# Experts' outputs made beside the row gather, and the gated sum of them fused into the stage that computes the gates

## The reference

```python
h = (x_flat @ W_gat).reshape(M, HEADS, NUM_EXPERTS)          # 4 heads x 4 experts
e = leaky_relu(a_src[src] + a_dst[dst], negative_slope=0.2)
ee = exp(e - e_max[dst]); alpha = ee / (denom[dst] + 1e-16)
agg = segment_sum(h[src] * alpha[:, :, None], dst) + b_gat
scores = layernorm(agg, ln_gamma, ln_beta).reshape(M, HEADS, NUM_EXPERTS).mean(1)
topk_s, topk_i = top_k(scores, 2); w = softmax(topk_s)
for ei in range(4):
    g = where(topk_i == ei, w, 0.0).sum(-1)
    hh = gelu(x @ W1[ei] + b1[ei])                             # 128 -> 256
    out = out + g[..., None] * (hh @ W2[ei] + b2[ei])          # 256 -> 128
```

## Time and profile before

| | us |
|---|---|
| median of 3 runs (19387.88 to 19430.43) | 19410.53 |
| profiled execution, first to last instruction (span) | 20574.0 |

### The profile page before, as it was taken

How to read it: one execution, slowest core, us unless ns; L and a number is a source line. 1 busy time by engine, 2 the same in 40 slices (tenths; PEclk the granted TensorE clock), 3 DMA queues, 4 the chain that set the end, 5 groups by cost and what they waited for, 6 DMA issues and landing times. The chain is left out here.

```text
span 20574.0 us, 221676 instructions
## 1 busy us (share of the span) xinstructions
PE 6617.7 (32%) x79074; PEld 3179.5 (15%) x79074; DVE 7802.0 (38%) x10945; ACT 3746.9 (18%) x6493; POOL 10631.0 (52%) x10003
## 2 busy tenths in 40 slices
PE   0298411000000000099799998720000000000079
PEld 0133210000000000043255554310000000000034
DVE  9987495110011111344588886411111110111244
ACT  0132210000000000034766665510000000000023
POOL 0023687777777777622100000367777777777710
PEclk9599655555555555599899999855555555555589
DMA  1011201211111111155211113421111111111145
GB/s 41 18 43 47 74 14 49 49 38 35 35 38 38 38 38 38 17 143 121 68 47 45 45 47 96 133 56 38 38 38 38 38 35 38 35 38 38 26 103 130
DMA packets 866809, 1073.12 MB, mean 52 GB/s; under 512 B 353908, under 2 KB 570069, under 8 KB 846421
## 3 DMA queue, kind: packets, MB, share of 16 engines
q1 hardware_dynamic: 413908, 612.28, 10.5%
q0 software_dynamic: 328768, 179.97, 6.5%
q10 hardware_dynamic: 123456, 270.60, 3.8%
HBM read 671.93 MB, written 390.08 MB: 52 GB/s over the span
## 5 line engine op out<-in xcount | busy, mean ns | idle before, releaser
L956 POOL DMA_INDIRECT g_got<-table,g_ring x8192 | 8981.6, 1096 | 2705.2 <-issue 2674.8
L1178 PE MATMUL g_rowsP<-g_eye,g_meta 128*20 128x128 f32 x12 | 2.9, 416 | 10731.0 <-DVEq L1222 10731.0
L1070 DVE TENSOR_TENSOR g_z<-g_gs,g_adm 128x512 f32<-128x512 f32 x64 | 44.0, 688 | 8585.4 <-DMA g_gs<-rows 7831.9
L1033 ACT ACTIVATE g_low<-g_z 128x512 f32<-128x512 f32 x64 | 38.5, 601 | 10365.5 <-issue 7495.1
L1178 PEld LDWEIGHTS g_rowsP<-g_eye,g_meta 128*20 128x20 f32 x12 | 1.5, 142 | 10731.6 <-DVEq L1222 10731.2
L2132 POOL DMA_DIRECT2D m_x<-x x64 | 34.4, 537 | 2457.6 <-issue 2451.2
L1419 PE MATMUL f_hP<-f_xn,f_w 128*128 128x512 f32 x2048 | 965.8, 594 | 647.9 <-DMA f_xn<-xn 647.9
L1426 PE MATMUL f_oP<-f_hid,f_w 128*128 128x512 f32 x2048 | 962.1, 592 | 0.0
L1450 ACT ACTIVATE f_hid<-f_hP,f_b 128x512 f32<-128x512 f32 x1024 | 648.7, 685 | 1120.4 <-PE f_hP L1419 1020.2
L1466 DVE SCALAR_TENSOR_TENSOR f_part<-f_oP,f_b,f_gate 128x512 f32<-128x512 f32 x512 | 384.6, 751 | 970.7 <-PE f_oP L1426 970.7
L905 POOL DMA_INDIRECT ad<-h_hs,k_start_row x512 | 503.4, 983 | 341.5 <-ACT h_hs L889 178.1
(11 more groups left out here) (412 smaller groups left out, 16112.7 us busy)
## 6 DMA issues: line engine op xcount, KB each, us to landing
g_got<-table,g_ring POOLq DMA_INDIRECT x8192
f_gate<-gates SPq DMA_DIRECT2D x128, 1024.0 KB
rows<-g_got SPq DMA_DIRECT2D x512, 192.0 KB
g_gs<-rows ACTq DMA_DIRECT2D x64, 1536.0 KB
state<-g_out ACTq DMA_DIRECT2D x64, 1536.0 KB
h_x<-x SPq DMA_DIRECT2D x128, 256.0 KB
xn<-h_xn ACTq DMA_DIRECT2D x128, 256.0 KB
f_xn<-xn SPq DMA_DIRECT2D x128, 256.0 KB
```

Source lines behind the costliest of these rows:

```text
L956: pool.indirect_dma_start(self.got[:,par,k,:],None,self.table,bass.IndirectOffsetOnAxis(ap=self.ring[:,par,k:k+1].bitcast(u32),axis=0)).th ...
```

## The change

A class `Experts` makes, beside the gather, the outputs of all four experts for every token, plus the bias, token-major, and stores them to a DRAM tensor `ffn` [32768, 512]. Each of the 32 slots of the gather does two expert tiles ahead of the gather tile on TensorE, ScalarE and VectorE; in layer 0 TensorE waits for the end of the sort. The totals stage then also loads `ffn` and x (three tiles ahead, SyncE), scales each 128 x 128 block by its gate on ScalarE, sums the four by matmuls against the identity in PSUM, adds x on VectorE and stores the result. Tiles are interleaved with the gate groups: group 0, tiles 0 to 3, group 1, tiles 4 to 19, group 2, tiles 20 to 35, group 3, tiles 36 to 63. The stage `experts` is gone, and with it the store and the broadcast loads of the gates. Token order within the totals changes to node = n x 128 + p, so the load of `nodes` is now of 96-byte rows and is issued from ScalarE's queue; `Bounds` transposes three tables instead of one, and for layer 1 it moves from the experts stage into the mamba core, as 128 turns of two.

```diff
+class Experts:
+    def tensor(self,pe,t,par,first):
+        for u in range(EX*2):
+            e,f=u//2,u%2
+            if not (first and u<2): pe.wait_ge(self.active,t*EX*2+u-1)
+            TE.matmul(self.hP[:,f,:],self.w1[:,e,f*P:f*P+P],self.xs[:,par,:],start=True,stop=True).then_inc(self.up,1)
+        pe.wait_ge(self.active,t*EX*2+EX*2)
+        for q in range(BLOCKS):
+            if not (first and q<2): pe.wait_ge(self.biased,t*BLOCKS+q-1)
+            for e in range(EX):
+                for f in range(2):
+                    last=TE.matmul(self.oP[:,q%2,e*P:e*P+P],self.hid[:,e,f,q*P:q*P+P],self.w2[:,e,f,:],start=(f==0),stop=(f==1),skip_group_check=True)
+            last.then_inc(self.down,1)
+    def vector(self,dve,t,par,early):
+        for q in range(BLOCKS):
+            dve.wait_ge(self.down,t*BLOCKS+q+1)
+            self.nc.vector.tensor_tensor(self.y[:,par,q,:],self.oP[:,q%2,:],self.b2[:,:],ALU.add).then_inc(self.biased,1)
...
+                def experts(i):
+                    for k in range(2):
+                        ex.scalar(act,i*2+k,k,begin and k==0)
+                        if not (begin and k==0): ex.store(act,i*2+k-1,1-k)
...
                 def tile(i,par):
+                    experts(i)
...
+            def tiles(body, group):
+                group(0)
+                for t in range(TILES):
+                    if t%GT==GT//4 and t//GT+1<HI//GROUP: group(t//GT+1)
+                    body(t)
...
+                for t in range(TILES):
+                    sp.wait_ge(added,t+1)
+                    sp.dma_start(x_out[:,t*T:(t+1)*T],xo[:,t%2,:]).then_inc(x_put[t%2],16)
+                    if t+AHEAD<TILES: load(t+AHEAD)
...
+                    for q in range(BLOCKS):
+                        j=t*BLOCKS+q
+                        pe.wait_ge(gated,j+1)
+                        for e in range(EX):
+                            last=nc.tensor.matmul(mixP[t%2][:,q*P:q*P+P],part[:,j%2,e,:],ident[:,:],start=(e==0),stop=(e==EX-1),skip_group_check=True)
+                        last.then_inc(mixed,1)
...
+                        if j>=2: act.wait_ge(mixed,j-1)
+                        for e in range(EX):
+                            last=nc.scalar.activation(part[:,j%2,e,:],yin[:,t%AHEAD,q,e*P:e*P+P],ACT.Copy,scale=gt[:,e,j:j+1])
+                        last.then_inc(gated,1)
...
+                def add(t):
+                    dve.wait_ge(mixed,(t+1)*BLOCKS)
+                    V.tensor_tensor(xo[:,t%2,:],mixP[t%2][:,:],xin[:,t%AHEAD,:],ALU.add).then_inc(added,1)
-def experts(nc, x, xn, gates, w1, b1, w2, b2, x_out, beside=None, tag="f"):
-                sp.dma_start(gt[:,par,:,:],gates[:,bass.ds(i*T,T)].partition_broadcast(P)).then_inc(g_in[par],16)
```

More of the change, by code:

```diff
@@ L918 @@
 GROUP=64
+EX=4
+FF=256
+BLOCKS=T//P
 class Gather:
@@ L968, in attention @@
+def attention(nc, keep, src, dst, ad, table, rows_d, state_d, bgat, gamma, beta, eye, x, xn, w1, b1, w2, b2, ffn, x_out, beside=None, tag="g"):
     with ExitStack() as ctx0:
@@ L1005, in attention, with slots @@
             str_=state_d.rearrange("(p c) f -> p c f",p=P)
+            def slots(eng, body):
+                for i in range(2): body(i,i)
+                with eng.Fori(1,N//2-1) as t:
+                    body(t*2,0)
+                    body(t*2+1,1)
+                for i in range(N-2,N): body(i,i%2)
             block=ctx.enter_context(nc.Block())
@@ L1042, in tile @@
                     nc.scalar.dma_start(str_[:,bass.ds(i*C,C),:],out[:,par,1:C+1,:]).then_inc(out_in[par],16)
-                paired(act,N,tile,peel=True)
+                slots(act,tile)
+                ex.store(act,TILES-1,1)
+                ex.stored(act)
+                act.wait_ge(nodes_in,16)
                 for s in out_in: act.wait_ge(s,N//2*16)
@@ L1093, in tile, with _ @@
                     summed.of(dve,i)
-                paired(dve,N,tile,peel=True)
+                slots(dve,tile)
                 V.tensor_copy(tail[:,:],out[:,1,C,:])
-            if order: block.tensor(order.tensor)
+            @block.tensor
+            def _(pe):
+                if order:
+                    order.tensor(pe)
+                    pe.wait_ge(ordered,1)
+                pe.wait_ge(ex.w_in,64)
+                def tile(i,par):
+                    for k in range(2): ex.tensor(pe,i*2+k,k,isinstance(i,int) and i==0 and k==0)
+                slots(pe,tile)
         with ExitStack() as ctx:
@@ L1140, in attention @@
             movedP=[r.pb(f"movedP{k}",[P,2,HI]) for k in range(2)]
+            AHEAD=3
+            yin=r.sb("yin",[P,AHEAD,BLOCKS,EX*P])
+            xin=r.sb("xin",[P,AHEAD,T])
+            part=r.sb("part",[P,2,EX,P])
+            xo=r.sb("xo",[P,2,T])
+            mixP=[r.pb(f"mixP{k}",[P,T]) for k in range(2)]
+            y_in=[r.sem(f"y_in{k}") for k in range(AHEAD)]
+            x_in=[r.sem(f"x_in{k}") for k in range(AHEAD)]
+            x_put=r.pair("x_put")
+            gated,mixed,added=r.sem("gated"),r.sem("mixed"),r.sem("added")
             p_in=r.sem("p_in")
@@ L1197, in _, with group @@
                 go(row[:,5:7,:],row[:,5:7,:],ACT.Exp)
-                for q in range(HI//GROUP):
+                def group(q):
                     go(x3[:,:,:,:],x3[:,:,:,:],ACT.Exp)
@@ L1650, in mamba_core @@
         YO=r.pb("YO",[P,T])
+        bounds=beside(Room(nc,ctx,tag+"b"),GP[:,0:3*P].rearrange("p (a b) -> p a b",b=P))
         w_in=r.sem("w_in")
@@ L1815, in _ @@
             by_image(pe,step)
+            bounds.tensor_shift(pe)
+            bounds.tensor_end(pe)
         @block.scalar
```

262 lines of the change are left out of this document (104 added, 158 removed).

## The result

The changed kernel takes 18091.39 us, median of 4 runs (18069.7 to 18103.26); the kernel before took 19399.21 in 4 runs beside it (19375.07 to 19430.43). The ratio is 0.9324, with a 95% interval of 0.9311 to 0.9338: 1308 us less, where 1067 were forecast.

What follows compares the result with a forecast made beforehand. Each stage has its own limit: POOL's fetches in the gathers, TensorE in the experts stages. Experts -1790, totals +588, gathers +75 and core +60 sum to -1067, from 19410.5 to about 18345 us, range 18020 to 18880.

Steps and rivals of the forecast that it cites:

- the likeliest case: Whole kernel: the forecast of about 18345 us itself, own range 18070 to 18750, 71 in 100.
- What bounds each stage: Gathers are set by POOL's fetches, experts stages by TensorE, totals paced by fetches; core is near TensorE's and VectorE's limits.
- Room in the slot: Gathers: two expert tiles plus the gather tile take some 107 us, under the 180 us of 128 fetches.
- Guests and fetches, +75: Both gathers: added stores and loads slow the fetches, 71 us, plus 4 for `nodes`; from 0 to twice +75.
- The +527 of the rival: Gathers: 512 bias additions on VectorE hold up fetches as the sort does, +527 us, 18870; 6 in 100.
- Totals, +588: Both totals: 136 us of groups, 64 tiles of 6.0 us and 8, 528 against 234 us, +294 a layer.
- the first of the three candidates: Totals: ScalarE as a tile's limit, 16 operations of 0.254 us, 4.1 us a tile.
- The core, +60: Mamba core: 128 `Bounds` turns add VectorE work and fetches hold it up, partly hidden; +60 us, 0 to 205.
- Sum and surplus: Whole kernel: terms sum to -1067 us, with the 1163.5 us of profiled span over median left unchanged.
- a tile at 5.2 us (not 10.9): Totals, rival: ScalarE and TensorE take turns, 10.9 us a tile instead of 6.0, +627, 18970; 8 in 100.
- The better case: Totals and core: a tile at 4.9 us or less and a hidden core, 18070 and below; 6 in 100.
- the slot could turn the sign: Gathers, rival: a slot over 180 us costs 64 us per us, gain gone at 197; 3 in 100.

Runs made afterwards that it cites:

- before_again: The kernel before, unchanged, profiled a second time: run 19433.25 us, profile span 19431.7 us.
- adds_psum: The changed kernel with four unused 128x512 VectorE additions, one operand in PSUM, ahead of each bias addition: 18079.47 us, ratio 0.9325.
- stores_twice: The changed kernel with each `ffn` tile stored a second time, to a DRAM tensor nothing reads: 18092.73 us, ratio 0.9326.
- split_ahead: The changed kernel with one of four scalings moved from ScalarE to VectorE and four load buffers instead of three: 18022.85 us, ratio 0.929.
- core_alone: The kernel before with only layer 1's `Bounds` moved from the experts stage into the mamba core: 19405.44 us against 19399.28, ratio 1.0004.
- room_over: The changed kernel with 28 unused additions, one operand in PSUM, ahead of each bias addition: 20008.73 us, ratio 1.0316.
- split: The changed kernel with one of each four scalings done by VectorE instead of ScalarE, three load buffers: 18146.71 us, ratio 0.9353.

## Why the prediction was right, and where its sizes were off

The time lies in the range, and in the likeliest case's own range (18070 to 18750), but only 21 us above its lower end. Every cost was put too high and none too low, so no two errors cancelled. The steps, with the windows' bounds between gather and totals and otherwise from a stage's first to its last instruction, against the second profile of before (19431.7 to 18098.8, a change of -1333):

| step | forecast | measured |
|---|---|---|
| experts stages removed | -1790 | -1794 |
| totals | +588 | +441 |
| gathers | +75 | +17 |
| core | +60 | +18 |
| rest | 0 | -15 |
| sum | -1067 | -1333 |

- **What bounds each stage.** Right. That TensorE's 882 us disappear in POOL's gather is shown by its window and by the unchanged fetch.
- **Room in the slot.** The mechanism was right, its size too large: 107 us were forecast, 55 for the experts' matmuls and 52 for the gather tile's chain. With a backlog, just after the sort, the state stores of the changed kernel lie 59 us apart. This is its ScalarE timeline there, and TensorE's behind it:

```profile
3401.67 0.35 ACTq L1125 DMA_DIRECT2D state<-g_out  x1
...
3460.39 0.37 ACTq L1125 DMA_DIRECT2D state<-g_out  x1
```

```profile
3462.98 7.59 PE L1004 MATMUL g0s_turn<-g_xn,g_w 128*128 128x512 f32 x12 [25.26 <-ACT g0s_ei L1018]
3471.42 7.41 PE L1010 MATMUL g0s_turn<-g_w,g0s_ei 128*128 128x128 f32 x64 [0.85 <-ACT g0s_ei L1018]
```

  A tile's matmuls take 15.7 us and not up to 27, and TensorE waits only 25 us between two slots. The 52 belonged to the shown execution: in the second profile such a chain takes 31 us (before_again), and 2 x 15.7 + 31 = 62 would have been close to the 59.
- **Guests and fetches, +75.** Over-sized. The step took 1.4 us for 3.3 MB from two windows of the earlier trace rows that differ by one fetch, which is their resolution, in an execution whose fetches of layer 1 took from 0.94 to 1.94 us each; in the second profile none takes over 0.97, and such windows hold 71 and 72 (before_again). The 1.10 of the earlier trace rows was of that execution too, and not the PSUM operand's: in adds_psum a fetch takes 0.945 in the mean. stores_twice shows that 134 MB cost nothing. The choice of the earlier trace rows over the earlier trace rows for the additions was right all the same, and adds_psum shows it with five times their number. The +527 of the rival was wrong even for operands in SBUF: 2048 such additions cost 64 us.
- **Totals, +588.** The three groups were forecast at 61, 38 and 37 us and measured at 61.0, 37.6 and 38.0; order and waits were as the order rows had it. The mis-sized term is the tile: 6.0 us against 5.2, 64 x 0.8 = 51 a layer. (The stage's part behind group 0 is 475 and 476 us, where 528 were forecast.) ScalarE was the limit, the first of the three candidates, which the forecast had at 4.1: the earlier trace rows gave 0.254 us for one of 24 evictions, and here 16 scalings take 5.03, 0.31 each. split_ahead, with 12 of them a tile, needs 4.6 us, so neither TensorE nor the queue set the 5.2. Nor were the DMA values of 4.9 and 6.6 us a floor: with a tile of 4.6 us in split_ahead, ScalarE waited 1.0 us for the loads in the whole stage. The other 22 a layer come from the baseline: 234 us after the first group in the shown execution, 256 in the second profile.
- **The core, +60.** Over-sized. VectorE's 61 us more are there, but for the most part hidden: core_alone shows +6 us of time with an interval from -12 to +25, and the +18 of the table is within what the stage differs by between executions. The 327 us that the forecast had free on VectorE were read from the window that ends early; the whole stage had 352, and TensorE 79 and not 60. The fetches' drag on VectorE was counted from a totals group, where VectorE's chain is exposed.
- **Sum and surplus.** The forecast left the 1163.5 us between span and median unchanged, with the reason that the removed stages are bound by matmuls. before_again shows that the reason holds (897 and 893 us against 898 and 895) and that the surplus lay almost all in the gathers, so the -1790 could be taken over in full.
- **The signs.** The removed stage and the gaps of 61, 38 and 38 us came as forecast. The gather of layer 1 was to take 5750 to 5830 us with a fetch near 1.4; it took 5169 with 1.25, much as the unchanged kernel's in its second profile (5161 with 1.25), so those two signs described the shown execution. TensorE is busy for a fifth of a slot (1021 of 5169 us) and not a third, the totals take 594 and 596 us and not 670, and the core 2507 and not 2460.
- **The rivals.** None of those with a loss came about: a tile at 5.2 us (not 10.9), a fetch at 1.25 (not above 1.5), a slot with 100 us of room. The better case, 18070 and below, was missed by 21 us: its core and gather terms came nearly as it said, its tile at 4.9 us did not. That the slot could turn the sign was right, as room_over shows, but its price was wrong: not 64 us for each us over 180. In layer 0 it counts from 140.5 us, since the sort delays the tiles, and so, by an estimate from these runs, the gain would be gone at (1308 + 31 x 140.5 + 32 x 161.5) / 63 = 172 us a slot.

## What to carry to other kernels

Work that bounds a stage of its own can cost next to nothing (here 8 or 9 us a gather) in a stage that another engine sets alone, as long as the guest's chain fits into a slot; count the slots from the point at which they really start. In a new pipeline size each engine and each queue for one tile and take the largest, then look at what else stands in the pacing engine's queue: letting tiles run inside the groups of 61, 38 and 38 us was worth 198 us here, more than the one choice of engine that gained (69, in split_ahead). Relieving the pacing engine shows the next limit, so give its loads a buffer more in the same step (124 us, from split to split_ahead). And where a profile's span lies 6% above the runs, take a second profile before terms are read from it: here a chain of 52 us was 31 in the second, and a fetch lost beside traffic was none.

## What the runs showed of the hardware

- The same kernel's fetch (128 rows, indirect, from GpSimd) has a period of 1.25 or 1.26 us in all these profiles but one, and of 1.40 in that: spans of 19431.7 and 20574.0 for one program. In that execution the two stages of heads were 46 and 38 us longer as well, and a tile's chain on VectorE and ScalarE took 52 us instead of 31, while the fetches of the totals (254.14 us for 256, against 253.37) and the two stages bound by matmuls (897 and 893 us, against 898 and 895) were as ever. The cause is open.
- The fetch does not feel 134 MB of other stores over two gathers of 5.5 and 5.2 ms (stores_twice: 0.944 us each in layer 1, against 0.946 in the changed kernel). Nor does it feel 7168 additions with one operand in PSUM in one gather (room_over, 0.944 us each). What moved it was VectorE with both operands in SBUF: to 1.97 us beside the sort's 1024-column operations back to back, to 1.05 and 1.41 in the rows shown beside bursts of four with 512 columns. What makes the difference between these two was not tried.
- A scaling of 128x128 with a scale for each partition takes 0.31 us on ScalarE (5.03 for 16), against 0.254 of the plain evictions in the earlier trace rows.
- The granted clock read 0.50 or 1.00 in 28 of the 31 windows of 1 us from 595 to 626 of the shown execution, and between the two in three. Sixteen records of the sort's matmuls (L409) took 1.97 us from 394.82 on, at a clock of 1.00, and 3.67 us from 866.77 on, at 0.50.
